# Two convolution layers on one core: the inverse transform's rows as an even and an odd half of 128 columns, put together by three engines

## The reference

```python
# layer 0: quantized 3x3 convolution
x = x + _L0_conv_ref(_gn(x), weight_int8, scale_weight, bias)
# layer 1: 3x3 complex convolution of the spectrum
X = jnp.fft.rfftn(_gn(x), axes=(-2, -1))
Yr = conv(Xr, wr) - conv(Xi, wi) + b_real
Yi = conv(Xr, wi) + conv(Xi, wr) + b_imag
x = x + jnp.fft.irfftn(Yr + 1j * Yi, axes=(-2, -1))
```

## Time and profile before

| | |
|---|---|
| median of 3 runs | 4113.66 us |
| the profiled execution | 4118.58 us, its span 4116.8 us |
| PE, matmuls | busy 3335.3 us (81%), 45732 instructions |
| DVE | busy 2828.5 us (69%) |
| ACT | busy 1884.1 us (46%) |
| POOL | busy 1492.8 us (36%) |
| mean granted clock of PE | 0.985 of full speed |

### The profile page before, as it was taken

One profiled execution on the slowest core, in us unless ns is written; L12 is line 12 of the kernel. 1 busy time (PEld: TensorE's weight loads), 2 busy tenths in 40 slices (PEclk: granted clock), 3 DMA queues, 4 the chain that ended last, 5 costly groups with the idle time before them and its releaser, 6 DMA issues.

```text
span 4116.8 us, 124636 instructions
## 1 busy us (share of the span) xinstructions
PE 3335.3 (81%) x45732; PEld 2923.3 (71%) x45732; DVE 2828.5 (69%) x4344; ACT 1884.1 (46%) x2767; POOL 1492.8 (36%) x1984
## 2 busy tenths in 40 slices
PE   0000018999999999999999999999999999999999
PEld 0000006888888888888888888888888888888888
DVE  8999974666666666666666666666666666666664
ACT  8999952334343333333343333333333333333333
POOL 5775002333333333333333333333333333333333
PEclk9999999999999999999999999999999999999999
DMA  8667621556555555555565555555555555555555
GB/s 305 240 236 242 234 83 59 171 171 180 176 171 172 168 174 176 174 175 174 173 182 180 171 173 174 173 172 171 177 173 176 174 164 173 173 173 170 175 160 169
DMA packets 631284, 731.76 MB, mean 178 GB/s; under 512 B 76816, under 2 KB 602608, under 8 KB 615312
## 3 DMA queue, kind: packets, MB, share of 16 engines
q1 hardware_dynamic: 483216, 589.37, 44.6%
q10 hardware_dynamic: 147456, 134.28, 11.9%
HBM read 263.23 MB, written 134.22 MB: 97 GB/s over the span
## 4 chain that ended last, share of the span: by engine, by line
PE 58%; SPq 18%; issue 11%; DMA 6%; DVE 5%; ACT 2%; ACTq 1%; POOL 0%; DVEq 0%; POOLq 0%
PE fin_ps L972 11%; PE y_ps L953 11%; PE mean_b L998 10%; SPq L436 10%; PE conv_ps L985 8%; PE x_ps L940 7%; SPq L358 6%; DMA img<-in_x 4%; PE t_ps L931 4%; PE conv_ps L987 3%; DVE scaled L733 2%; PE fin_ps L967 2%; DMA halo<-quant 2%; SPq L425 1%; DVE scaled L734 1%
## 5 line engine op out<-in xcount | busy, mean ns | idle before, releaser
L704 POOL TENSOR_SCALAR eo<-img,norm 128x256 f32<-128x256 f32 x512 | 484.6, 946 | 1882.5 <-PE t_ps L931 1732.3
L953 PEld LDWEIGHTS y_ps<-mix_w,stack 128*128 128x128 f16 x24576 | 784.1, 99 | 90.8 <-DMA stack<-xn 13.1
L953 PE MATMUL y_ps<-mix_w,stack 128*128 128x64 f16 x24576 | 800.9, 193 | 9.2 <-DMA stack<-xn 9.0
L518 ACT ACTIVATE xt<-t_ps 128x512 f32<-128x512 f32 x512 | 305.7, 597 | 1095.7 <-PE t_ps L931 802.1
L972 PE MATMUL fin_ps<-inv,y_hi 128*128 128x256 f16 x4096 | 750.5, 279 | 0.0
L796 DVE SCALAR_TENSOR_TENSOR xn<-x_ps,norm,xn 128x512 f16<-128x512 f32 x512 | 384.2, 750 | 403.7 <-ACT xn L525 399.5
L511 ACT ACTIVATE scaled<-img,b,a 128x512 f32<-128x512 f32 x512 | 413.6, 808 | 486.0 <-DMA img<-in_x 379.3
L809 DVE SCALAR_TENSOR_TENSOR img<-conv_ps,cst,img 128x512 f32<-128x512 f32 x512 | 383.6, 749 | 284.3 <-PE conv_ps L987 271.1
L972 PE MATMUL fin_ps<-inv,y_lo 128*128 128x256 f16 x2048 | 570.5, 279 | 0.0
L998 PE MATMUL mean_b<-row_mean,img 128*128 128x48 f32 x4096 | 537.9, 275 | 12.7 <-DVE img L809 12.7
L940 PE MATMUL x_ps<-dft,xt 128*128 128x128 f32 x4096 | 545.2, 276 | 2.1 <-DVE xn L796 2.1
...
## 6 DMA issues: line engine op xcount, KB each, us to landing
...
halo<-quant SPq DMA_DIRECT2D x192, 193.3 KB, 3.3
...
```

Source lines behind the costliest of these rows:

```text
L704: nc.gpsimd.tensor_scalar(even, rows[:, :, 0:F], norm[v][:, 2:3], None, ALU.add).then_inc(shift_s, 1)
L953: last = nc.tensor.matmul(y_ps[t % 2][:, g, b, :], stack[:, t % 2, g, first:first + F], mix_w[:, 2 * at + b, g, f, part, :], start=i == 0, ...
```

## The change

The values that leave the inverse transform for columns w and 255-w are a sum and a difference of the same two numbers: a part that is even about the row's middle (from the real coefficients) and one that is odd (from the imaginary ones). The table `inv` now holds 128 columns instead of 256. The 6 matmuls of a block write 3 times the even half and 3 times the odd half of `fin_ps` (L1026 after). Then:
- ACT's new `odd_out(t)` copies the odd half, scaled, to SBUF, at the end of the slot, before the store.
- DVE's `finish_pair(t)` waits for it (`odd_s`) and adds the even half to the left half of the image's row and, mirrored, to its right half: two instructions of 128 x 256.
- POOL's new `unfold(t)` adds the odd part to the left half and subtracts it from the mirrored right half: two instructions of 128 x 256. It stands in slot t+1 behind `fold(t+5)`. The last one of a sample, `unfold(15)`, stands at the end of slot 15.
- `store(t)` waits for POOL (`done_s`) and stands in ACT's slot t+2 instead of t+1; the last two of a sample are issued in the next period.

The edge rows' `finish_rows` gets 128 columns too and stands on PE behind `finish_pair(15)`. `scale_pair` waits for its own pair (`pair_s`) instead of a quarter. On SP the load of pair t-3 stands ahead of `restack(t+3)`; it was the load of pair t-2 behind it. The loop's body is 7 times two samples instead of 3, and two samples are written out ahead of it.

```diff
-TURN = 3
+PEEL = 1
+TURN = 7
...
-        inv = sb("inv", [P, 2, 2, N], f16)
+        inv = sb("inv", [P, 2, 2, F], f16)
...
+        odd_part = sb("odd_part", [P, 2, 2, F])
...
-        fin_ps = pb("fin_ps", [P, 2, N])
+        fin_ps = pb("fin_ps", [P, 2, 2, F])
...
                 for t in range(PAIRS):
+                    if mix and t >= 3 and ahead:
+                        sp.wait_ge(store_s[(t - 3) % STORES], stored(s, t - 3))
+                        sp.sem_inc(tick_s, 1)
+                        load_pair(s + 2, u, t - 3)
...
                     if runs(mix, conv, t + 3):
                         restack(s, t + 3)
-                    if mix and t >= 2 and ahead:
-                        sp.wait_ge(store_s[(t - 2) % STORES], stored(s, t - 2))
...
-                act.wait_ge(load_s[u][j // QP], loaded(SP2 - 1) + 16 * NQ * i + (64 if u == 1 and j // QP == QU - 1 else 0))
+                if not (isinstance(i, int) and i == 0):
+                    act.wait_ge(pair_s[u][j], 32 * i + 1)
...
+            def odd_out(s, t):
+
+                act.wait_ge(fin_s, done(s, t))
+                act.wait_ge(done_s, done(s, t - 2))
+                nc.scalar.activation(odd_part[:, t % 2], fin_ps[:, :, 1, :], ACT.Copy, scale=1.0 / FIN).then_inc(odd_s, 1)
...
-                        nc.scalar.activation(im_f[:], image_ps, ACT.Identity, bias=image_b).then_inc(imf_s, 1)
-                    if mix and t >= 1:
-                        store(s, u, t - 1)
-                if mix:
-                    store(s, u, PAIRS - 1)
+                        nc.scalar.activation(im_f[:, 0:F], image_ps[:, 0, :], ACT.Identity, bias=image_b)
+                        nc.scalar.activation(im_f[:, F:N], image_ps[:, 1, :], ACT.Copy).then_inc(imf_s, 1)
+                    if mix:
+                        odd_out(s, t)
+                    if mix and t >= 2:
+                        store(s, u, t - 2)
+                    if later(s, mix) and t < 2:
+                        store(s - 1, 1 - u, t + PAIRS - 2)
...
+            def unfold(s, u, t):
+
+                rows, odd = img[u][:, 2 * t:2 * t + 2, :], odd_part[:, t % 2]
+                near, far = rows[:, :, 0:F], rows[:, :, N - 1:F - 1:-1]
+                pool.wait_ge(even_s, done(s, t))
+                pool.sem_inc(tick_s, 1)
+                pool.wait_ge(odd_s, done(s, t))
+                pool.sem_inc(tick_s, 1)
+                nc.gpsimd.tensor_tensor(near, near, odd, ALU.add)
+                nc.gpsimd.tensor_tensor(far, far, odd, ALU.subtract).then_inc(done_s, 1)
...
                     if runs(mix, conv, t + 4):
                         fold(s, u, t + 4)
+                    if mix and t >= 1:
+                        unfold(s, u, t - 1)
                     if conv and t == STATS_AT + 1:
                         pool.wait_ge(veps_s, s + 2)
...
+                if mix:
+                    unfold(s, u, PAIRS - 1)
...
-                dve.wait_ge(fin_s, done(s, t))
-                nc.vector.scalar_tensor_tensor(rows, fin_ps[:], 1.0 / FIN, rows, ALU.mult, ALU.add).then_inc(done_s, 1)
+                near, far = rows[:, :, 0:F], rows[:, :, N - 1:F - 1:-1]
+                even = fin_ps[:, :, 0, :]
+                dve.wait_ge(odd_s, done(s, t))
+                nc.vector.scalar_tensor_tensor(near, even, 1.0 / FIN, near, ALU.mult, ALU.add)
+                nc.vector.scalar_tensor_tensor(far, even, 1.0 / FIN, far, ALU.mult, ALU.add).then_inc(even_s, 1)
...
-                pe.wait_ge(done_s, done(s, t - 1))
+                pe.wait_ge(even_s, done(s, t - 1))
+                pe.wait_ge(odd_s, done(s, t - 1))
...
-                            last = nc.tensor.matmul(to, y[:, t % 2, 2 * b + q].rearrange("p x g -> p (x g)"), inv[:, q, part, :],
+                            last = nc.tensor.matmul(fin_ps[:, b, q, :], y[:, t % 2, 2 * b + q].rearrange("p x g -> p (x g)"), inv[:, q, part, :],
...
+                    if mix:
+                        finish_pair(s, t)
                     if conv and t == IMAGE_AT + 3:
                         finish_rows(s + 1)
-                    if mix:
-                        finish_pair(s, t)
```

More of the change, by code:

```diff
@@ L72, in shape_tables @@
     tab["ident"] = np.eye(P)
-    ang = th * np.outer(k, h - mid)
+    ang = th * np.outer(k, h[:F] - mid)
     weight = np.full((F + 1, 1), 2.0)
@@ L271, in build @@
         iy_ps = misc_ps[:, 0:96].rearrange("p (t x) -> p t x", t=2)
-        image_ps = misc_ps[:, 192:448]
+        image_ps = misc_ps[:, 192:448].rearrange("p (q w) -> p q w", q=2)
         stat_ps = misc_ps[:, 452:456]
         load_s = [[sem(f"load{i}{q}") for q in range(QU)] for i in range(2)]
+        pair_s = [[sem(f"pair{i}_{j}") for j in range(PAIRS)] for i in range(2)]
         halo_s = [sem(f"halo_s{q}") for q in range(QU)]
@@ L307, in periods @@
             period(-1, 1, False, True, True)
-            with engine.Fori(0, (SP2 - 1) // TURN) as j:
-                for v in range(TURN):
-                    for u in range(2):
-                        period(TURN * j + v, u, True, True, True)
-            for v in range((SP2 - 1) // TURN * TURN, SP2 - 1):
+            rounds = (SP2 - 1 - PEEL) // TURN
+            for v in range(PEEL):
+                for u in range(2):
+                    period(v, u, True, True, True)
+            if rounds:
+                with engine.Fori(0, rounds) as j:
+                    for v in range(TURN):
+                        for u in range(2):
+                            period(TURN * j + v + PEEL, u, True, True, True)
+            for v in range(PEEL + rounds * TURN, SP2 - 1):
                 for u in range(2):
@@ L320, in runs, with later @@
             return mix if t < PAIRS else conv
+        def later(s, mix):
+            return mix and not (isinstance(s, int) and s == 0)
         def done(s, t):
@@ L352, in _, with load, load_pair @@
         def _(sp):
-            def load(k, u, q, rs=range(QB)):
+            def load(k, u, q):
                 src = x[k].rearrange("c (h r) w -> c r h w", r=R)
-                for r in rs:
+                for r in range(QB):
                     sp.dma_start(img[u][:, QB * q + r, :], src[:, :, QB * q + r, :]).then_inc(load_s[u][q], 16)
+            def load_pair(k, u, j):
+                src = x[k].rearrange("c (h r) w -> c r h w", r=R)
+                for hb in (2 * j, 2 * j + 1):
+                    sp.dma_start(img[u][:, hb, :], src[:, :, hb, :]).then_inc(pair_s[u][j], 16)
             def load_runs(k, u, q):
@@ L464, in _ @@
                 sp.sem_inc(store_s[b], 1)
+            for u in range(2):
+                for j in range(PAIRS):
+                    sp.sem_inc(pair_s[u][j], 1)
             for c in range(2):
@@ L474, in _ @@
             act.sem_inc(p1_act, 8)
-            for q in (t1e_s, xhi_s, yhi_s):
+            for q in (t1e_s, xhi_s, yhi_s, odd_s):
                 act.sem_inc(q, LEAD)
@@ L577, in _ @@
             periods(act, period)
+            for t in (PAIRS - 2, PAIRS - 1):
+                store(samples - 1, 1, t)
         @block.gpsimd
@@ L582, in _ @@
             pool.sem_inc(fold_s, LEAD)
+            pool.sem_inc(done_s, LEAD)
             setup = Tally(pool, setup_p)
@@ L723, in _ @@
         def _(dve):
-            for q in (xlo_s, ylo_s, done_s, x1_s):
+            for q in (xlo_s, ylo_s, even_s, x1_s):
                 dve.sem_inc(q, LEAD)
@@ L1042, in finish_rows @@
                     for i, (y, part) in enumerate(((iy_hi, 0), (iy_hi, 1), (iy_lo, 0))):
-                        last = nc.tensor.matmul(image_ps, y[:, q].rearrange("p d x -> p (d x)")[:, 0:P], inv[:, q, part, :],
-                                                start=q == 0 and i == 0, stop=q == 1 and i == 2)
+                        last = nc.tensor.matmul(image_ps[:, q, :], y[:, q].rearrange("p d x -> p (d x)")[:, 0:P], inv[:, q, part, :],
+                                                start=i == 0, stop=i == 2)
                 last.then_inc(imps_s, 1)
```

19 lines of the change are left out of this document (9 added, 10 removed).

## The result

The changed kernel takes 4167.0 us (median of 4 runs, 4162.5 to 4188.6), the kernel before 4113.9 (4 runs, 4112.1 to 4124.7). The ratio is 1.013 [1.009, 1.017]: 1.3% slower, where 4030 us and faster had been forecast, and outside both ranges (3980 to 4085, and 3930 to 4150 for 8 in 10). The profiled execution took 4169.8 us, its span 4168.0, at a mean granted clock of 0.958 (0.985 before).

The account below looks back on a forecast made before the run. PE was taken as the bound; slots with the new chain's stops summed to 105.1 us a period against 107.7, 81 us over 31 periods, with 9 off for the loop and 3 added: 4030 us, range 3980 to 4085.

Parts of the forecast that it names:

- the price of a matmul: PE's inverse transform: a matmul of 128 columns takes 55 ns instead of 109, 0.66 us less a slot.
- the load waits: ACT's scale_pair: its 3.70 us wait for a load goes, and with it PE's idle time before finish_rows.
- the new chain: fin(t) through ACT, DVE and POOL to turn(t+6): 5.35 us; PE stands 3.4 at slot 12, 5.8 at the seam.
- Slots 4 to 9: Slots with two convolutions: 7.07 us each, 42.4 together, with ACT's queue taken as hidden in the short slots.
- Slot 10: 6.07 less 0.66 us, plus 0.5 because DVE reaches the statistics later behind its longer finish.
- Slot 12: After a 3.4 us stop, half a chance of 2.6 us from a low clock, half of it hidden: 0.7.
- Slot 15 and seam: finish_rows 0.4 us late behind x_high on ACT, then PE stands 5.8 us for fold(4) behind unfold(15).
- Slot 0: Low clock behind the seam's stop adds 2.6 us to 4.8: slot 0 takes 7.4.
- PE as the bound: Rival, chance 0.06: POOL keeps ahead, a period is PE's own work, 90 us; 3560 us in all.
- The clock: Rival, chance 0.2: the chain is there but the clock stays up at both stops, 3.3 us less a period, about 3930.
- POOL and DVE slow each other: Rival, chance 0.17: POOL's chain instructions are held, unfold gains 0.36 and the fold 0.5 us; about 4160.
- weight loads don't hide: Rival, chance 0.05: PE's matmuls of 128 columns take 82 ns, 4.2 us a period more; 4160 us.

Follow-up runs that it names:

- e1: Changed kernel with unfold(15) moved behind the next period's fold of pair 4: 3971.6 us, 0.965 to the kernel before.
- e14: Changed kernel with the store ahead of odd_out on ACT only in slots 4 to 9: 4105.5 us, 0.999 to the kernel before.
- e3: Changed kernel with the store ahead of odd_out on ACT in every slot: 4203.7 us, 1.023 to the kernel before.
- e6: The e5 kernel with the store ahead of odd_out in every slot: 3839.9 us, 0.933 to the kernel before.
- e5: Changed kernel with unfold(t-2) in slot t, across the seam too, and the power ahead of it: 3884.2 us, 0.944 to the kernel before.
- e7: The e5 kernel with unfold's two additions left out, POOL only counting the semaphore: 3883.7 us.
- e12: Changed kernel with 28 unused matmuls of 416 columns keeping PE at work in the seam's stop: 4122.5 us, 1.002 to the kernel before.
- e11: The e5 kernel with each of a slot's 12 inverse matmuls issued twice: 4080.8 us, 0.995 to the kernel before.
- e13: The e5 kernel with store early in slots 4 to 9, restack before load, row_low before finish_pair(13), halo first on SP in slots 2 and 6: 3761.0 us.

## Why the prediction was wrong, step by step

**Right: the price of a matmul.** 55 ns were forecast. The chain of waits has six in 0.33 to 0.34 us, 55 to 57 ns, each with its own weight load. By the rule of the Trainium skill, "TensorE: Matmul & The Clock Gate", section "Back-to-back issue gap" (about 81 ns each in such a stream), the six would take 0.49 us, an estimate; the trace disagrees.

```profile
2122.45 0.11 PE fin_ps L1021
2122.56 0.34 PE fin_ps L1026 x6
2122.89 0.11 PE fin_ps L1021
```

**Right: the load waits go, and the new chain takes their place.** The timeline of ACT, DVE and POOL at the seam answers to the earlier trace rows:

```profile
2211.44 0.37 ACT L597 ACTIVATE im_f<-misc_ps,cst 128x128 f32<-128x128 f32 x1 [0.57 <-PE misc_ps L1097]
2211.71 0.27 ACT L598 ACTIVATE im_f<-misc_ps 128x128 f32<-128x128 f32 x1
...
2211.87 0.39 ACT L561 ACTIVATE odd_part<-fin_ps 128x256 f32<-128x256 f32 x1
...
2212.29 0.43 DVE L869 SCALAR_TENSOR_TENSOR img<-fin_ps,img 128x256 f32<-128x256 f32 x1 [0.77 <-ACT odd_part L561]
...
2212.63 0.41 DVE L870 SCALAR_TENSOR_TENSOR img<-fin_ps,img 128x256 f32<-128x256 f32 x1
...
2213.32 0.72 POOL L752 TENSOR_TENSOR img<-img,odd_part 128x256 f32<-128x256 f32 x1 [3.94 <-DVE img L870]
...
2214.00 0.91 POOL L753 TENSOR_TENSOR img<-img,odd_part 128x256 f32<-128x256 f32 x1
...
2214.89 0.96 POOL L739 TENSOR_SCALAR eo<-img,norm 128x256 f32<-128x256 f32 x1
...
2216.50 0.72 POOL L742 TENSOR_TENSOR eo<-eo,img 128x256 f32<-128x256 f32 x1
```

`odd_out` 0.39 (forecast 0.38), DVE's even half 0.75 (0.88), unfold 1.57 (1.42), fold 2.33 (2.30). Each link is in place and near the forecast's size, and e1 confirms the cause. The stop of 5.8 is 5.9 in most periods (6.0 in the mean), that of 3.4 is 3.1 to 3.5.

**Wrong: what the change does to the slots that were taken as covered.** Measured between the first and the last sample, a period lasts 109.5 us, not 105.1; 31 times 4.4 are 136 of the 138 us by which the profiled execution missed 4031.6. The terms, from the table:

*Slots 4 to 9, +3.0: the term that failed most.* The prediction took them as before less 12 matmuls (42.4 us) and put ACT's queue down as hidden. It never priced that the store now stands between `odd_out`, which waits for the end of fin(t), and the next `turn_out`. ACT from the end of slot 5 into slot 6, in the changed kernel:

```profile
2148.41 0.38 ACT L561 ACTIVATE odd_part<-fin_ps 128x256 f32<-128x256 f32 x1 [2.10 <-PE fin_ps L1026]
2148.61 1.47 ACTq L569 DMA_DIRECT2D out<-img  x2
2150.18 0.60 ACT L541 ACTIVATE xt<-t_ps 128x512 f32<-128x512 f32 x1 [1.39 <-PE x_ps L993]
2150.67 0.68 ACT L548 ACTIVATE xn<-x_ps,norm 128x512 f16<-128x512 f32 x1
```

In the kernel before, the store's issue was over 2.7 us before `turn_out` had anything to do:

```profile
2154.49 1.31 ACTq L540 DMA_DIRECT2D out<-img  x2
2158.53 0.60 ACT L518 ACTIVATE xt<-t_ps 128x512 f32<-128x512 f32 x1 [3.65 <-PE t_ps L931]
```

Now it starts behind fin(t), takes 1.5 us, and `x_high`, DVE's `x_low` and `layer0_pair` (L859) come late for PE's `row_means` (L1052 in the groups above). The "idle" that ends with `x_ps` is the issue's time. e14, e3 and e6 take the store off this place and get 43.0, 42.7 and 42.8 us: 2.4 to 2.7 of the 3.0 hang on the store's place, and that is shown.

Slot 7 alone holds 1.6 of the 3.0: 8.65 us where 7.07 were forecast. The prediction read 7.73 us from one slot and took it for all six, but slot 7 of the kernel before lasts 8.40 in the mean, since PE waits there for the quantized image's halo; with that reading its sum would have had 0.7 more, of which its unplaced 0.3 may hold a part. In all (first figure, 23 of it once at the start) PE waits for the halo, before and after:

```profile
PE conv_ps L985 <- DMA halo<-quant: 39.2, 25, 23.3
PE conv_ps L1039 <- DMA halo<-quant: 48.1, 17, 23.4
```

In e14 slot 7 takes 7.2 us. SP issues the halo behind a load that waits for the store; that a late store makes the halo late by this way is argued, not shown. Of the others slot 4 lasts 7.38 us there, the rest 7.10 to 7.13.

*Slot 10, +0.9.* The prediction had 0.5 for DVE's longer finish. Beyond that, the small instructions of the statistics now run beside POOL's unfold and fold. DVE and then POOL:

```profile
2180.33 0.57 DVE L878 TENSOR_TENSOR small<-small,cst 128x1 f32<-128x1 f32 x1
...
2181.87 0.63 DVE L886 TENSOR_TENSOR small<-small 128x1 f32<-128x1 f32 x1
```

```profile
2180.16 0.72 POOL L753 TENSOR_TENSOR img<-img,odd_part 128x256 f32<-128x256 f32 x1
...
2181.75 0.73 POOL L740 TENSOR_TENSOR eo<-img 128x256 f32<-128x256 f32 x1
```

One value per partition takes 0.57 us and ends at 2180.90, where POOL's instruction ends at 2180.88; the second ends at 2182.50, POOL's at 2182.48. Before, the same instruction (L825 there) took 0.16 us. In e5, where POOL stands idle at that moment, it takes 0.16 again (L881 there) and slot 10 lasts 6.1, in e7 6.2. So 0.7 of the 0.9 is shown.

*Slot 12, +0.7.* I had given the lower clock half a chance. In 22 of 30 periods the granted clock is low in the slot and it lasts 5.4 to 6.8 us; in the 8 others the clock is at full and it lasts 4.05. The stop beforehand is 3.08 to 3.47 us in the 22 and 3.08 to 3.19 in the 8. One period after the rows above it shows in L1059, 0.93 instead of 0.54 us:

```profile
2298.34 0.66 PE L984 MATMUL t_ps<-ident,eo 128*128 128x128 f32 x4 [3.47 <-POOL eo L742]
2299.96 0.93 PE L1059 MATMUL mean_b<-channel,norm 128*128 128x48 f32 x4
```

*Slot 15 and seam, +0.95.* `finish_rows` waits 0.7 us for DVE's `iy_lo` (22.0 us in all, group above), where the forecast had 0.4; the stop at the seam is 6.0 in the mean instead of 5.8, and 0.1 is a wait for `stack<-xn`. The rest, 0.35, I can't place.

*Slot 0, -0.8.* The lower clock behind the seam costs 1.7 us (6.6 against 4.9 in e12), not the 2.6 that the prediction took from the earlier trace rows: half of the stretch at the lower level falls into the stop, where PE has no work (2214.10 to 2217.34 in the window above), and 3.6 us of it fall on work.

Slots 1 to 3, 11, and 13 with 14 came out within 0.2 us. The loop was worth 11 us (9 forecast), the last sample costs 5.3 (71.9 us from the last start of the impulse to the end, for 66.6 in the earlier trace rows; 3 forecast).

**The rivals.** PE as the bound at 3560 was far off: even with the chain taken away, 96 us a period is the best that was reached, and doubling showed that two fifths of the saved columns are off the path. The clock doesn't stay up: it was low behind the stop at the seam in all 31 periods, and in slot 12 in 22 of 30. "POOL and DVE slow each other" and "weight loads don't hide" both gave 4160, close to the 4167 measured, but that is luck: the unfold's two additions take 0.725 and 0.736 us in the mean, the fold's three 0.937, 0.745 and 0.733 (0.946, 0.737 and 0.742 before), so POOL is not held, e7 shows that the additions cost nothing in e5's order, and only slot 10's small instructions are held. Weight loads hide, at 55 to 57 ns.

**The change by parts.** Against the finer waits alone (103.3 us a period) the halves bring 2.9 us where POOL's order is right (e5, 100.4). That is a sum of two: the columns saved are worth 6.2 (e11, 106.5), and all that comes with them costs 3.2. With the queues of ACT, SP and DVE in order too it is 7.1 (e13, 96.2); how much of this the same queue orders would bring with 256 columns was not measured. In the order of the change the halves cost 6.3, more than the 4.3 that the load waits bring.
